# Keys of image tokens by seven products instead of eight, in an fp32 cross-attention kernel

## The reference, cut to what matters

```python
q = _heads(hidden_states @ to_q_w)                       # x: (16, 512, 640), 20 heads of 32
h_txt = _sdpa(q, _heads(ehs_txt @ to_k_w), _heads(ehs_txt @ to_v_w))          # tokens 0..76
h_obj = _sdpa(q, _heads(ehs_obj @ to_k_object_w), ...)                        # 77..80
h_oth = _sdpa(q, _heads(ehs_oth @ to_k_others_w), ...)                        # 81..84
h_ip = _sdpa(q, _heads(ehs_ip @ to_k_ip_w), _heads(ehs_ip @ to_v_ip_w))       # 85..511
out = _merge(h_txt) + _merge(h_obj) + _merge(h_oth) + _merge(h_ip)
out = out @ to_out_w + to_out_b + residual
```

## Time and profile before

| what | us |
|---|---|
| three runs, median (lowest to highest) | 2381.95 (2381.77 to 2382.32) |
| the profiled execution's own time | 2381.67 |
| its span, first to last instruction | 2379.5 |
| TensorE busy | 2365.9 |
| VectorE busy | 1835.2 |
| ScalarE busy | 1775.6 |
| GpSimd busy | 412.5 |

### The profile page before, as it was taken

The page is one execution under the profiler, slowest core; times in us unless marked ns, Lnnn a source line. Parts: engine busy times, 40 slices in busy tenths (PEclk is TensorE's granted clock), DMA queues, the critical chain, the costliest instruction groups (busy, mean ns, idle before and its releaser), DMA issues.

```text
span 2379.5 us, 37663 instructions
## 1 busy us (share of the span) xinstructions
PE 2365.9 (99%) x12801; PEld 1805.1 (76%) x12801; DVE 1835.2 (77%) x3291; ACT 1775.6 (75%) x3906; POOL 412.5 (17%) x564
## 2 busy tenths in 40 slices
PE   9999999999999999999999999999999999999999
PEld 8999999998999986566666666666666666666665
DVE  4457777732333489999999999999999999999994
ACT  4343433332223369999999999999999999999995
POOL 0000000000000023413223133133132231231310
PEclk9999999999999999999999999999999999999999
DMA  9445444374644555545555555555455555555542
GB/s 339 161 128 159 150 136 141 109 268 147 232 167 174 182 174 153 148 129 154 152 143 146 134 148 159 137 146 151 128 156 154 134 150 141 144 161 128 147 132 78
DMA packets 371749, 370.12 MB, mean 156 GB/s; under 512 B 110046, under 2 KB 298590, under 8 KB 371558
## 3 DMA queue, kind: packets, MB, share of 16 engines
q1 hardware_dynamic: 334384, 306.14, 46.7%
q10 hardware_dynamic: 37174, 61.59, 7.0%
HBM read 215.57 MB, written 83.89 MB: 126 GB/s over the span
## 4 chain that ended last, share of the span: by engine, by line
PE 97%; ACT 2%; issue 0%; DMA 0%; DVE 0%; ACTq 0%
PE st_ps L1661 17%; PE s_ps L489 13%; PE st_ps L509 12%; PE om_ps L523 12%; PE om_ps L544 11%; PE om_ps L567 11%; PE s_ps L1713 7%; PE om_ps L1713 4%; PE s_ps L1681 3%; PE st_ps L1713 3%; ACT s_ps L689 1%; PE om_ps L1730 1%; ACT probs L681 1%; PE om_ps L602 1%; PE st_ps L1621 0%
## 5 line engine op out<-in xcount | busy, mean ns | idle before, releaser
L689 ACT ACTIVATE s_ps<-s_ps,negmax 128x427 f32<-128x427 f32 x1280 | 767.8, 608 | 21.6 <-DVE small L759 21.6
L750 DVE TENSOR_REDUCE negmax<-s_ps 128x2 f32<-128x854 f32 x640 | 666.0, 1041 | 75.4 <-PE s_ps L489 69.1
L681 ACT ACTIVATE probs<-st_ps 128x1024 f32<-128x1024 f32 x632 | 656.1, 1038 | 15.2 <-PE st_ps L509 3.7
L489 PE MATMUL s_ps<-kpack,qpack 96*128 96x512 f32 x1280 | 420.9, 410 | 2.1 <-ACT s_ps L689 2.1
L509 PE MATMUL st_ps<-qpack,kpack 104*128 104x512 f32 x1264 | 405.4, 402 | 2.5 <-ACT probs L681 2.5
L447 POOL TENSOR_TENSOR small<-small,negmax 128x616 f32<-128x616 f32 x160 | 196.5, 1228 | 999.8 <-DVE negmax L767 999.6
L1661 PE MATMUL st_ps<-ctx_split,w_split_ip 128*128 128x428 f32 x1848 | 364.2, 358 | 0.0
L1661 PEld LDWEIGHTS st_ps<-ctx_split,w_split_ip 128*128 128x128 f32 x1848 | 347.4, 188 | 15.2 <-issue 1.0
L489 PEld LDWEIGHTS s_ps<-kpack,qpack 96*128 96x128 f32 x1280 | 223.4, 189 | 177.6 <-ACT s_ps L689 81.0
L544 PE MATMUL om_ps<-xs,wq 128*128 128x512 f32 x1200 | 340.6, 394 | 0.0
L567 PE MATMUL om_ps<-heads,wo 128*128 128x512 f32 x1125 | 320.8, 394 | 0.0
(11 more groups left out here) (116 smaller groups left out, 2437.8 us busy)
## 6 DMA issues: line engine op xcount, KB each, us to landing
qpack<-q_out SPq DMA_DIRECT2D x240, 256.0 KB, 4.7
kpack<-kT SPq DMA_DIRECT2D x240, 217.5 KB, 2.9
kT<-k_out ACTq DMA_DIRECT2D x154, 217.5 KB, 3.3
ctx_split_raw<-in_ctxT SPq DMA_DIRECT2D x128, 214.0 KB, 4.6
tok_pair<-in_ctxT SPq DMA_DIRECT2D x48, 512.0 KB, 4.7
xs_raw<-in_xT SPq DMA_DIRECT2D x85, 256.0 KB, 3.8
out<-in_xT SPq DMA_DIRECT2D x75, 256.0 KB, 4.0
out_yT<-out SPq DMA_DIRECT2D x75, 256.0 KB, 2.1
```

What stands on the lines that cost most here:

```text
L489: last = nc.tensor.matmul(s_ps[:, n % 2, z, :], qpack[r][0:ROWS_S, j, t * P:(t + 1) * P], kpack[r][0:ROWS_S, j, :], start=True, stop=True)
L681: nc.scalar.activation(probs[:, at:at + 2, :], transposed(u, duo), ACT.Exp).then_inc(p_done, 1)
L689: last = nc.scalar.activation(s_ps[:, n % 2, z, SMALL:TOK], s_ps[:, n % 2, z, SMALL:TOK], ACT.Exp, bias=negmax[:, r, IP, j, t:t + 1], accu ...
L750: nc.vector.tensor_reduce(negmax[:, r, IP, j, t0:t0 + 2], s_ps[:, n % 2, :, SMALL:TOK], AX_X, ALU.max, negate=True).then_inc(s_max, 1)
```

## The change

Batches 3 to 10 are taken in four pairs (`K_PAIRS`). Of a pair, the first four blocks of 128 key channels of both batches are one 2x2 by 2x2 problem: the context's halves of channels (k = 0, 1) and the two batches (h) give B11, B21 (batch one, first and second half of the channels), B12 and B22 (batch two); the weights' halves give the sums S1 to S4. Seven products take the place of eight, each of two groups (t = 0, 1) of 12 matmuls of 128x428. The fifth block of each batch is made as before (kind "F"). That makes 18 groups of 12 matmuls for a pair (`K_GROUPS`), where ten blocks of 24 stood.

The operands of a pair, in the order in which they are used, are B11, T3, T2, T4, B21, T1, B22, B12, with T3 = B22 - B12, T2 = T3 + B11, T4 = B21 - T2, T1 = B12 - B11. GpSimd makes the four sums (`key_sum`, 128x1712 each, at steps 16 of the pair ahead, 0, 3 and 7; in pair 0 the first two at blocks 3 and 4 of batch 2). Each operand is split in one piece of 128x1712 by ScalarE and VectorE into one of three slots, so that its split waits for the product three operands back. Products share PSUM banks: X and Q in `s_ps`, U in `om_ps`, F in `st_ps`. VectorE adds them (`add_group`: two additions behind each of groups 5 and 6, one behind each of 7, 8, 12 to 15), and within a step an addition stands ahead of the low part of an earlier block, and that ahead of splits. Group 7 waits for the additions behind group 5, group 8 for those behind group 6.

Stores of these 40 blocks go out on SP's queue (`store_group`) instead of ScalarE's; the raw context of the next pair but one is loaded by four DMAs of 128x4x428 (`load_raw`) between the stores of groups 14 and 15. The weights' sums are made by VectorE in batch 2 (four additions and four splits of 128x1024) from quarters that SP loads again. The two small products `("s", 2, 0)` and `("s", 3, 0)` stand one batch earlier, and the loads of the first queries' operands behind the pairs instead of within batch 5. The diff, cut:

```diff
+K_PAIRS = ((3, 4), (5, 6), (7, 8), (9, 10))
+K_PAIRED = tuple(b for pair in K_PAIRS for b in pair)
+K_OPERANDS = (B11, T3, T2, T4, B21, T1, B22, "B12")
...
+K_GROUPS = ((0, "X", 0), (0, "X", 1), (0, "F", 0), (1, "Q", 0), (1, "Q", 1), (2, "U", 0), (2, "U", 1),
+            (3, "Q", 0), (3, "Q", 1), (4, "X", 0), (4, "X", 1), (4, "F", 0), (5, "U", 0), (5, "U", 1),
+            (6, "U", 0), (6, "U", 1), (6, "F", 1), (7, "F", 1))
+K_OUT = {7: (0, 2), 8: (0, 3), 9: (0, 0), 10: (0, 1), 11: (0, 4), 12: (1, 2), 13: (1, 3), 14: (1, 0), 15: (1, 1), 17: (1, 4)}
+K_OUT_ORDER = tuple(K_OUT.values())
+U_ADDS = 10
...
-        ORDER += [("k", run, m) for m in k_slots(run)]
-        ORDER += {TXT + 1: [("s", 2, 0)], TXT + 2: [("s", 3, 0)]}.get(run, [])
+        if run - TXT not in K_PAIRED:
+            ORDER += [("k", run, m) for m in k_slots(run)]
+        elif K_PAIRED.index(run - TXT) % 2 == 0:
+            ORDER += [("p", K_PAIRED.index(run - TXT) // 2, i) for i in range(len(K_GROUPS))]
+        ORDER += {TXT: [("s", 2, 0)], TXT + 1: [("s", 3, 0)]}.get(run, [])
...
+    SUMS[("k", before_pairs, 0)] = ("sw", 0)
+    for m, parts in ((1, (S3, S2)), (2, (S1, S4))):
+        SPLITS.setdefault(("k", before_pairs, m), []).extend(("sw", i, 0) for i in parts)
+    for pp in range(len(K_PAIRS)):
+        ahead = [("k", before_pairs, 3), ("k", before_pairs, 4)] if pp == 0 else [("p", pp - 1, 15), ("p", pp - 1, 17)]
+        for j, step in enumerate(ahead + [("p", pp, i) for i in (2 if pp else 0, 3, 6, 9, 11, 13)]):
+            SPLITS.setdefault(step, []).append(("z", pp, j))
+    T_SUMS = {}
+    for pp in range(len(K_PAIRS)):
+        ahead = [("k", before_pairs, 3), ("k", before_pairs, 4)] if pp == 0 else [("p", pp - 1, 16), ("p", pp, 0)]
+        for i, step in zip((T3, T2, T4, T1), ahead + [("p", pp, 3), ("p", pp, 7)]):
+            T_SUMS[step] = (i, pp)
...
+    def stage_done(engine, z):
+
+        pp, j = divmod(z, len(K_OPERANDS))
+        if j in (0, 1, 6):
+            engine.wait_ge(z_acc, 3 * pp + {0: 1, 1: 2, 6: 3}[j])
+        elif j == 2:
+            engine.wait_ge(u_acc, 4 * pp + 4)
+        else:
+            engine.wait_ge(k_acc, pair_base(pp) + {3: 2, 4: 5, 5: 7, 7: 10}[j])
...
+        def store_group(pp, i):
+
+            run, m = pair_block(pp, i)
+            k0 = k_num(run, m)
+            sp.wait_ge(k_lo, k0 + 1)
+            sp.wait_ge(k_fill, k0 - k_base(TXT) + 1)
+            for part in (HI, LO):
+                sp.dma_start(d["kT"][run - TXT, part, m * P:(m + 1) * P, N_TXT:TOK],
+                             k_out[:, k0 % KR, part, 0:SM + IPN - 1].bitcast(F32)).then_inc(k_stored[k0 % KR], 16)
...
+        def load_raw(pp):
+
+            if pp < 2:
+                sp.wait_ge(k_acc, k_base(before_pairs + pp))
+            else:
+                sp.wait_ge(piece_lo, split_upto(("z", pp - 2, len(K_OPERANDS) - 1)))
+            for h, k in ((0, 0), (1, 1), (1, 0), (0, 1)):
+                sp.dma_start(raw[pp % 2][:, h, k, :, :],
+                             d["ctxT"][K_PAIRS[pp][h], k * CC2 * P:(k + 1) * CC2 * P, TOK - IPN:TOK]
+                             .rearrange("(n p) t -> p n t", p=P)).then_inc(raw_in[pp % 2][h][k], 16)
...
+        for pp in range(len(K_PAIRS)):
+            for i in K_OUT:
+                store_group(pp, i)
+                if i == 14:
+                    if pp + 2 < len(K_PAIRS):
+                        load_raw(pp + 2)
+                    else:
+                        for n in range(CC):
+                            load_c(K_LOAD[behind_pairs + pp + 2 - len(K_PAIRS)], n)
...
+            elif kind == "z":
+                i, z = K_OPERANDS[n], z_number(which, n)
+                if z < K_SLOTS:
+                    act.wait_ge(s_acc, 4)
+                    act.wait_ge(sv_stored, 32)
+                else:
+                    stage_done(act, z - K_SLOTS)
+                if i in T_ORDER:
+                    act.wait_ge(t_raw, summed(i, which))
+                else:
+                    h, k = {B11: (0, 0), B21: (0, 1), B22: (1, 1), "B12": (1, 0)}[i]
+                    act.wait_ge(raw_in[which % 2][h][k], raw_landed(which))
...
+        def keep_group(pp, i):
+            run, m = pair_block(pp, i)
+            k0, (to, at, n) = k_num(run, m), k_cols(run)
+            _, kind, t = K_GROUPS[i]
+            if kind in "QU":
+                act.wait_ge(u_add, U_ADDS * pp + {7: 5, 8: 6, 12: 7, 13: 8, 14: 9, 15: 10}[i])
+            else:
+                act.wait_ge(k_acc, k0 + 1)
+            act.wait_ge(k_stored[k0 % KR], stored_upto(k0 % KR, k0))
+            src = u3_k[:, t, :] if i in (12, 13) else bank(pp, kind, t)
+            nc.scalar.activation(k_out[:, k0 % KR, HI, to:to + n], src[:, at:at + n], ACT.Copy).then_inc(k_hi, 1)
...
+        def add_group(pp, i):
+
+            _, kind, t = K_GROUPS[i]
+            u2, u3, n = u2_k[:, t, :], u3_k[:, t, :], U_ADDS * pp
+            if i in (5, 6):
+                dve.wait_ge(u_acc, 4 * pp + t + 3)
+                dve.wait_ge(x_sb, 2 * pp + t + 1)
+                if pp > 0:
+                    dve.wait_ge(u_add, n)
+                    dve.wait_ge(k_lo, pair_base(pp) - 3)
+                nc.vector.tensor_tensor(u2, bank(pp, "U", t), u2, ALU.add).then_inc(u_add, 1)
+                dve.wait_ge(u_add, n + 2 * t + 1)
+                nc.vector.tensor_tensor(u3, bank(pp, "Q", t), u2, ALU.add).then_inc(u_add, 1)
+            elif i in (7, 8, 14, 15):
+                k0 = k_num(*pair_block(pp, i))
+                dve.wait_ge(k_acc, k0 + 1)
+                dve.wait_ge(u_add, n + (4 if i < 10 else 8))
+                nc.vector.tensor_tensor(bank(pp, kind, t), bank(pp, kind, t), u2, ALU.add).then_inc(u_add, 1)
+            elif i in (12, 13):
+                dve.wait_ge(k_acc, k_num(*pair_block(pp, i)) + 1)
+                dve.wait_ge(u_add, n + 4)
...
+            dve.wait_ge(k_hi, k0 + 1)
+            nc.vector.tensor_tensor(k_out[:, k0 % KR, LO, to:to + n], src[:, at:at + n],
+                                    k_out[:, k0 % KR, HI, to:to + n].bitcast(F32), ALU.subtract).then_inc(k_lo, 1)
...
+            if kind == "p":
+                add_group(a, b)
+                if b - 1 in K_OUT:
+                    keep_group(a, b - 1)
+                if b == len(K_GROUPS) - 1:
+                    keep_group(a, b)
...
+            if i == T3:
+                if pp == 0:
+                    pool.wait_ge(s_acc, 4)
+                    pool.wait_ge(sv_stored, 32)
+                else:
+                    pool.wait_ge(piece_lo, split_upto(("z", pp - 1, 1)))
+                pool.wait_ge(raw_in[pp % 2][1][1], raw_landed(pp))
+                pool.wait_ge(raw_in[pp % 2][1][0], raw_landed(pp))
+                to, a, b, op = t3_raw[:, :, :], b22, b12, ALU.subtract
+            elif i == T2:
+                if pp > 0:
+                    pool.wait_ge(piece_lo, split_upto(("z", pp - 1, 2)))
+                pool.wait_ge(t_raw, summed(T3, pp))
+                pool.wait_ge(raw_in[pp % 2][0][0], raw_landed(pp))
+                to, a, b, op = t2_raw[:, :, :], t3_raw[:, :, :], b11, ALU.add
+            elif i == T4:
+                stage_done(pool, z_number(pp, 3) - K_SLOTS)
+                pool.wait_ge(t_raw, summed(T2, pp))
+                pool.wait_ge(raw_in[pp % 2][0][1], raw_landed(pp))
+                to, a, b, op = z_raw(pp, 3), b21, t2_raw[:, :, :], ALU.subtract
+            else:
+                stage_done(pool, z_number(pp, 5) - K_SLOTS)
+                to, a, b, op = z_raw(pp, 5), b12, b11, ALU.subtract
+            nc.gpsimd.tensor_tensor(to, a, b, op).then_inc(t_raw, 1)
...
+            j, kind, t = K_GROUPS[i]
+            base, z = pair_base(pp), z_number(pp, j)
+            if i == 0 or K_GROUPS[i - 1][0] != j:
+                pe.wait_ge(piece_lo, split_upto(("z", pp, j)))
...
+                else:
+                    pe.wait_ge(k_lo, base - 1)
+            elif i in (7, 8):
+                pe.wait_ge(u_add, U_ADDS * pp + 2 * (t + 1))
+            elif i in (9, 10):
+                pe.wait_ge(u_add, U_ADDS * pp + 2 * t + 1)
+            elif i in (14, 15):
+                pe.wait_ge(u_add, U_ADDS * pp + 7 + t)
+            elif i == 16:
```

More of the change, by code:

```diff
@@ L1006, in landed @@
     def landed(load):
-        return 16 * sum(buffer(n) == buffer(load) for n in range(load + 1))
+        return 16 * sum(buffer(n) == buffer(load) and LOAD_RUN[n] - TXT not in K_PAIRED for n in range(load + 1))
     def is_txt(run):
@@ L1043, in k_base, with k_num @@
         return run * QC
+    def k_num(run, m):
+        b = run - TXT
+        if b not in K_PAIRED:
+            return k_base(run) + m
+        first, second = K_PAIRS[K_PAIRED.index(b) // 2]
+        return k_base(TXT + first) + K_OUT_ORDER.index((b - first, m))
     K_ALL = k_base(RUNS) - DEFER
@@ new lines, in z_raw, with bank @@
+    def z_raw(pp, j):
+        i, (b11, b21, b12, b22) = K_OPERANDS[j], (raw[pp % 2][:, h, k, :, :] for h in range(2) for k in range(2))
```

(49 more changed lines are left out.)

133 lines of the change are left out of this document (116 added, 17 removed).

## The result

| what | before | after |
|---|---|---|
| median of 20 runs each (lowest to highest) | 2382.49 (2381.65 to 2383.30) | 2385.60 (2384.96 to 2386.63) |
| ratio to before, 95% interval | | 1.0014 (1.0007 to 1.0020) |
| span of the profiled execution | 2379.5 | 2384.6 |
| mean granted TensorE clock over the span | 1.000 | 0.997 |

The change makes the kernel 3.1 us slower, a difference under 0.2%. The forecast was 2384.6.

The account below looks back on a forecast made before the run. TensorE was taken to bound the kernel, busy 2365.9 of 2379.5 us. Removed matmuls -18.7, stops +20.0 and weight loads behind them +1.3 gave +2.6 us: 2384.3, or 2384.6 as a median; range 2371 to 2392.

Parts of the forecast that it names:

- What is removed: In the four pairs, 96 fewer TensorE matmuls of 128x428 at 0.1952 us each: 18.7 us saved, all on the path.
- A sum's duration: One GpSimd sum of 128x1712 takes 3.83 us, from two rows of operations on two full tensors.
- rival 2: Turns, but GpSimd sums of only 3.03 us, from the row with a spread operand: 2374 us; chance 10%.
- Turns: GpSimd sums and VectorE splits, both reading SBUF, exclude each other for whole instructions; whoever waited goes first; stops total 20.0 us.
- Rival 1: No turns: GpSimd sums and VectorE splits run beside each other, leaving small stops at group 7: 2364 us; chance 12%.
- its one place in the trace: At 848.49 us two VectorE splits took 2.14 us beside a GpSimd operation, for 1.12 together otherwise; read as turns.
- The seam: Between pairs, TensorE's group 3 is 4.0 us late, group 5 1.0 to 1.1, group 9 1.2: 6.3 a seam.
- A restart behind a stop: TensorE loads weights before multiplying again: 0.19 us behind each of seven stops, 1.3 us in all.
- rival 4: TensorE's clock falls to 1.2 GHz in the long stops; three groups at half pace add 7.0 us: 2392; chance 8%.
- Cost nothing: Stores on SP's queue, VectorE's weight sums in batch 2 and moved loads delay nobody; up to 1 us a pair if landings double.
- Rival 3: GpSimd keeps its turn, T4 going ahead of T3's split: group 3 7.9 us late, 2393 us; chance 5%.

Follow-up runs that it names:

- Experiment 4: The change with all sums made by VectorE, T3 and T2 of the next pair both at step 16: 2364.90 us, ratio 0.9925 to the kernel before.
- experiment 1: The change with a pair's four sums made by VectorE instead of GpSimd, at the same steps: 2368.65 us, ratio 0.9941 to the kernel before.
- experiment 2: The change with each GpSimd sum replaced by three constant writes that read nothing, sums left out: 2368.48 us.
- experiment 7: The change with each GpSimd sum replaced by two copies of one operand, sums left out: 2371.77 us.
- experiment 5: The change with the split of B21 one step sooner, step 5 in place of 6: 2378.89 us, ratio 0.9988 to the kernel before.
- experiment 3: The change with fifteen unread 128x256 matmuls on TensorE ahead of group 3 of pairs 1 to 3: 2383.38 us.
- experiment 6: The change with the pairs' stores issued by ScalarE again, one step behind their block: 2396.34 us, ratio 1.0060 to the kernel before.

## Why the prediction was right, point by point

- **What is removed, 18.7 us.** Held. The eight batches took 960 x 0.1952 = 187.4 us before and take 190.87, of it 864 x 0.1952 = 168.7 of matmuls at full pace and 22.2 of losses. Experiment 4, without stops, is 17.7 us faster over all.
- **A sum's duration.** 3.83 forecast, 3.9 measured. The line through the two rows of the same kind held; the row with a spread operand would have misled (rival 2, 3.03).
- **Turns.** Held, and shown by experiments 1, 2 and 7: 17 us of the change's time hang on GpSimd's sums reading SBUF while VectorE splits. By the rule of the Trainium skill (SBUF — State Buffer, "Who interferes with whom"), which the forecast weighed against its one place in the trace, the runs agree: splits of 5.4 us beside sums. Rival 1 falls.
- **The seam.** Group 3 is 3.45 late for 4.0: each step up to it came some 0.2 to 0.5 sooner than counted. Group 9 is 1.30 to 1.38 late for 1.2, and experiment 5 shows that the cause is the order in the queue, as written. Group 5, forecast 1.0 to 1.1 late, was not late at all, because the clock had slowed the groups ahead of it; with the clock held (experiment 3) it is 0.85 late. A restart behind a stop, put at 0.19, costs 0.1: the 24 matmuls from 640.22 take 4.80 us to the start of the next, at 645.02.
- **The clock.** Here the step failed that took rival 4 for an alternative with 8%: it came true together with the forecast. Stops of 3.45 us brought the clock to 1.2 GHz, though the first 4.80 us of the program, idle, had read 1.00. The page that the forecast named for it (the Trainium skill, TensorE: Matmul & The Clock Gate, "Why this matters for your kernels") states that a long enough pause brings the lower clock. The trace after agrees (0.50 behind a stop of 3.26), the first seam of experiment 5 does not: there a stop of 3.33 left the clock at 1.00. Rival 4's price of 7.0 was nearly that of the slow groups (6.1), but it did not take off the stop that they cover; net it was 3.1 in the traces and 2.2 by the medians. By luck this made up for the shorter stops: they sum to 15.6 for the 20.0 forecast, with 0.4 of restarts for 1.3, and the slow groups add 6.1 where the forecast had nothing, about 22.2 in all for 21.3. That the time came out 1.0 from the forecast owes in part to this.
- **Cost nothing.** The stores on the sync queue, the weights' sums and the loads made nobody wait in the trace; stores landed in 2.4 us (80 of them, median; 4.6 in the first seam, beside the raw loads). What the forecast did not see is how much the old place of the stores would have cost in this kernel, 10.7 us.
- **Rival 3**, GpSimd keeping its turn, falls: T4 asked at 621.42 and the waiting split went first, in all three seams.

## What to carry to other kernels

Before work is given to an idle GpSimd, look at what VectorE does at that moment: a VectorE instruction with both inputs in SBUF and a GpSimd one that reads SBUF took turns here, whole instruction by whole instruction, so that a long GpSimd instruction made a VectorE one that was needed next late by nearly its whole length; here the same sums on the busier VectorE, at half the duration, were 17 us faster. Work out stops of TensorE with the clock in them: one of 3.3 us was followed here, more often than not, by several us at half pace, which also hides smaller stops behind it. And a store that waits for two engines does not belong in the queue of an engine whose next work TensorE needs.

## What the runs showed of the hardware beyond the forecast

- GpSimd writing SBUF does not shut out VectorE (splits of 1930 to 1944 ns beside constant writes, experiment 2), GpSimd reading one input does (3.06 us, experiment 7).
- The turns hit short operations hardest in proportion: the copy of 128x16 went from 0.20 to as much as 1.76 us beside a split.
- The same stop, 3.3 us, was followed by a lower clock or was not, in one and the same execution (experiment 5); stops of 1.54 us and less never were in the profiled executions. Groups 3 and 4 then take between 1.5 and 2.9 us longer (the least and the most in experiments 6 and 5), and a stop that comes later is shorter by part of that.
